# Attention and a quantised product on one core: the beginning rebuilt (decay factors by way of TensorE, first rows in halves)

## The reference

```python
q = x @ Wq; k = x @ Wk; v = x @ Wv
latent_kv = (k + v) @ W_down_kv            # 128 -> 32
k_rec = latent_kv @ W_up_k                 # 32 -> 128
v_rec = latent_kv @ W_up_v
scores = clip(einsum(qh, kh) * scale)      # scale = 1/sqrt(128)
decay = exp(-0.01 * 0.01 * abs(i - j))
scores = clip(scores * decay)
attn = softmax(scores)                     # over keys
out = (attn @ vh) @ Wo
x = x + attention(layernorm(x))
x = x + (fp8(layernorm(x) / s_in) @ fp8(kernel / s_k)) * (s_in * s_k) + bias
```

## Time and profile before

| | us |
|---|---|
| median of 3 runs (lowest, highest) | 534.98 (530.42, 535.65) |
| profiled execution, its own time | 534.09 |
| its span | 532.2 |
| TensorE busy with matmuls | 490.4 |
| ScalarE busy | 490.8 |
| VectorE busy | 280.6 |
| GpSimd busy | 218.8 |
| first exponential of scores begins at | 15.58 |

### The profile page before, as it was taken

One profiled execution on the slowest core, in us unless ns is written; L12 is line 12 of the kernel. 1 busy time (PEld: TensorE's weight loads), 2 busy tenths in 40 slices (PEclk: granted clock), 3 DMA queues, 4 the chain that ended last, 5 costly groups with the idle time before them and its releaser, 6 DMA issues.

```text
span 532.2 us, 9397 instructions
## 1 busy us (share of the span) xinstructions
PE 490.4 (92%) x3457; PEld 113.2 (21%) x3457; DVE 280.6 (53%) x641; ACT 490.8 (92%) x534; POOL 218.8 (41%) x285
## 2 busy tenths in 40 slices
PE   7799999899999999999999999999999999999961
PEld 3312111131122212221121211221111212122220
DVE  4524744455645564554744555554555645455646
ACT  3789999889999999999999999999999999999961
POOL 0889419791450229992251218993101211002110
PEclk9999999899999999999999999999999999999995
DMA  5589789837976102757967000757977000100000
GB/s 174 166 253 223 254 240 261 315 144 175 249 158 149 46 5 71 263 183 192 263 149 178 10 4 23 278 169 214 264 176 166 20 7 7 46 1 2 1 20 25
DMA packets 50467, 73.79 MB, mean 139 GB/s; under 512 B 6192, under 2 KB 29168, under 8 KB 50416
## 3 DMA queue, kind: packets, MB, share of 16 engines
q1 hardware_dynamic: 49600, 72.85, 49.5%
q10 hardware_dynamic: 816, 0.28, 0.2%
HBM read 35.40 MB, written 35.65 MB: 133 GB/s over the span
## 4 chain that ended last, share of the span: by engine, by line
PE 45%; ACT 34%; issue 9%; DVE 5%; DMA 3%; POOL 2%; SPq 1%; ACTq 0%; DVEq 0%; POOLq 0%
ACT probs L758 33%; PE ps L957 23%; PE ps L941 13%; DVE ps L1182 2%; PE ps L937 2%; PE ps L859 1%; PE ps L854 1%; PE ps L822 1%; PE ps L831 1%; DMA decay<-decay_rows 1%; PE ps L826 1%; DMA o_raw<-pv_out 1%; DMA wuv_s<-L_attn_W_up_v 1%; SPq L453 0%; POOL sq L584 0%
## 5 line engine op out<-in xcount | busy, mean ns | idle before, releaser
L758 ACT ACTIVATE probs<-ps 128x1024 f32<-128x1024 f32 x512 | 480.2, 1067 | 14.9 <-DVE ps L1182 9.4
L957 PE MATMUL ps<-probs,V 128*9 128x512 f32 x2048 | 268.6, 596 | 3.0 <-ACT probs L758 0.8
L1182 DVE TENSOR_TENSOR ps<-ps,consts 128x256 f32<-128x256 f32 (+1 forms) x256 | 143.9, 565 | 176.3 <-PE ps L941 169.3
L941 PE MATMUL ps<-Qs,Ks 64*128 64x512 bf16 x992 | 181.7, 386 | 16.6 <-ACT probs L758 8.4
L941 PEld LDWEIGHTS ps<-Qs,Ks 64*128 64x128 bf16 x992 | 43.9, 93 | 288.8 <-ACT probs L758 272.1
L645 POOL TENSOR_TENSOR xs<-xs,magic 128x512 f32<-128x512 f32 x7 | 8.9, 1277 | 96.2 <-DVE magic L1243 96.2
L957 PEld LDWEIGHTS ps<-probs,V 128*9 128x9 f32 x2048 | 31.3, 88 | 77.9 <-issue 57.6
L1190 DVE COPY pv_out<-ps 105x512 f32<-105x512 f32 x31 | 21.4, 691 | 33.7 <-PE ps L957 33.7
L562 POOL TENSOR_SCALAR rs<-mv 128x4 f32<-128x4 f32 (+1 forms) x10 | 2.3, 229 | 82.7 <-DVEq L1364 82.0
L596 POOL TENSOR_TENSOR sq<-sq,parts 128x1024 f32<-128x1024 f32 (+1 forms) x16 | 29.0, 1813 | 1.3
L598 POOL TENSOR_TENSOR parts<-sq,parts 128x1024 bf16<-128x1024 f32 (+1 forms) x16 | 28.3, 1771 | 1.3
(11 more groups left out here) (148 smaller groups left out, 284.7 us busy)
## 6 DMA issues: line engine op xcount, KB each, us to landing
Qs<-qp_dram SPq DMA_DIRECT2D x26, 512.0 KB, 9.2
qp_dram<-parts SPq DMA_DIRECT2D x14, 768.0 KB, 4.6
Ks<-kp_dram SPq DMA_DIRECT2D x26, 384.0 KB, 5.5
kp_dram<-parts SPq DMA_DIRECT2D x12, 384.0 KB, 3.5
kp_dram<-parts SPq DMA_DIRECT2D x6, 768.0 KB, 5.2
qp_dram<-parts SPq DMA_DIRECT2D x7, 512.0 KB, 6.0
X<-L_attn_x SPq DMA_DIRECT2D x10, 256.0 KB, 3.3
Qs<-qp_dram SPq DMA_DIRECT2D x10, 256.0 KB, 9.5
```

Source lines behind the costliest of these rows:

```text
L758: nc.scalar.activation(probs[:, quad % RING, 2 * jp:2 * jp + 2, :].rearrange("p j n -> p (j n)"), ps_all[:, bank * CH:(bank + 2) * CH], AC ...
L941: last = nc.tensor.matmul(bank, Ks[half, g, jp, key_cols(v, kc)], Qs[half, g, jp, qh, v, :], start=True, stop=True)
L957: last = nc.tensor.matmul(pv[32 * j:32 * j + VW, :], V[:, unit // 2 * NB + kc, HG * j + g, :], probs[:, quad % RING, j, :], start=i == 0, ...
L1182: nc.vector.tensor_tensor(own, own, factors, ALU.mult).then_inc(fixed, 1)
```

## The change

It touches the beginning only.

- `decay` is no longer spread by two broadcast loads. One row of 2048 factors is loaded to one partition (`factors`, which lies in the tile `probs`; `factors_in`), as the third issue of SyncE's queue. TensorE multiplies it with a row of 128 ones in three pieces of 512 columns (f32, one row deep), and ScalarE copies the three accumulators to `decay` (`spread_factors` on both engines; `factors_ps`, `decay_ready`). The fourth piece, needed only by GpSimd's `late_keys`, is still a broadcast load, of 256 KB instead of 1 MB (`decay_in`).
- The first four row tiles arrive as two loads, one on SyncE's queue and one ahead of the weights on ScalarE's (`x_quarter`). They get moments, square root, inversion and normalisation of their own, ahead of the second four; the last two tiles of the second four are normalised between `first_queries` and `first_keys`.
- `keep_busy` is 8 instead of 11, and those of 3 and 5 are gone.
- The table of the exponential is loaded after the copy of the first `xnT` and the third `spread_factors`, and the square root of the second four rows stands before that copy. The two late weight loads of ScalarE's queue move behind it.
- `load_x(1)` waits for `consts` instead of for `decay`.
- TensorE waits for the third copy of factors before slot 1, since it writes over its accumulator.

```diff
@@ sync
-            sp.dma_start(X[:, 0, 0:4, :], x_t[:, 0:4, :]).then_inc(x_half, 16)
+            sp.dma_start(X[:, 0, 0:2, :], x_t[:, 0:2, :]).then_inc(x_quarter[0], 16)
             sp.dma_start(X[:, 0, 4:NB, :], x_t[:, 4:NB, :]).then_inc(x_in[0], 16)
+            sp.dma_start(factors[:, :], decay_rows[:, :]).then_inc(factors_in, 16)
...
-            for half in range(2):
-                cols = slice(half * CH, (half + 1) * CH)
-                sp.dma_start(decay[:, :, cols], decay_rows.rearrange("o (a n) -> o a n", a=2)[:, :, cols]
-                             .broadcast_to([P, 2, CH])).then_inc((decay_half, decay_in)[half], 16)
-            sp.wait_ge(decay_half, 16)
-            sp.wait_ge(decay_in, 16)
+            sp.dma_start(decay[:, 1, CH:S], decay_rows[:, S + CH:2 * S].broadcast_to([P, CH])).then_inc(decay_in, 16)
+            sp.wait_ge(const_in, 16)
             load_x(1)
@@ gpsimd
-            pool.wait_ge(decay_in, 16)
+            pool.wait_ge(decay_ready, 3)
             pool.wait_ge(k_sb, 2)
...
             split(0, CH, CH)
+            pool.wait_ge(decay_in, 16)
             late_keys(0)
@@ scalar
+            act.dma_start(X[:, 0, 2:4, :], x.rearrange("(t p) d -> p t d", p=P)[:, 2:4, :]).then_inc(x_quarter[1], 16)
             act.dma_start(wkT_s[:, :], wkT[:, :]).then_inc(w_in, 16)
...
-            deviation(0, mv, rs)
+            def spread_factors(i):
+                v, half = FACTORS[i]
+                act.wait_ge(factors_ps, i + 1)
+                nc.scalar.copy(decay[:, v, half * CH:(half + 1) * CH], ps[:, 1 + i, :]).then_inc(decay_ready, 1)
+
+            deviation(0, mv[:, first_rows, :], rs[:, :, first_rows])
+            spread_factors(0)
+            spread_factors(1)
             act.wait_ge(fold_pe, 1)
             nc.scalar.copy(wdown_T[:, :], ps[0:DL, 7, 0:D]).then_inc(fold_act, 1)
-
-            nc.scalar.activation(unread[:, 1:2], ones[:, :], ACT.Exp, scale=SCALE)
             act.wait_ge(fold_pe, 2)
             nc.scalar.copy(wk_eff[:, :], ps[:, 6, 0:D]).then_inc(fold_act, 1)
             nc.scalar.copy(wv_eff[:, :], ps[:, 6, D:2 * D]).then_inc(fold_act, 1)
+            deviation(1, mv[:, second_rows, :], rs[:, :, second_rows])
+            act.wait_ge(tr_ps, 1)
+            nc.scalar.copy(xnT[:, 0:CH], ps[:, 4, :]).then_inc(xnT_ready, 1)
+            spread_factors(2)
+            nc.scalar.activation(unread[:, 1:2], ones[:, :], ACT.Exp, scale=SCALE)
@@ tensor
+            def spread_factors(i):
+                at = FACTORS[i][0] * S + FACTORS[i][1] * CH
+                nc.tensor.matmul(ps[:, 1 + i, :], one_row[:, :], factors[:, at:at + CH], start=True,
+                                 stop=True).then_inc(factors_ps, 1)
+
             pe.wait_ge(tiles_clear, 1)
-            keep_busy(11)
+            keep_busy(8)
+            pe.wait_ge(factors_in, 16)
+            spread_factors(0)
+            spread_factors(1)
...
-            keep_busy(3)
+            spread_factors(2)
...
-            keep_busy(5)
@@ vector
-            dve.wait_ge(x_half, 16)
-            tile_stats(0, range(4))
+            for i in range(2):
+                dve.wait_ge(x_quarter[i], 16)
+                tile_stats(0, range(2 * i, 2 * i + 2))
+            tile_moments(range(4))
+            settle()
+            dve.sem_inc(var_ready, 1)
             dve.wait_ge(x_in[0], 16)
             tile_stats(0, range(4, NB))
-            tile_moments(range(NB))
+            invert_deviation(0, mv[:, first_rows, :], rs[:, :, first_rows])
+            normalise_first(range(4)).then_inc(xn_ready[0], 1)
+            tile_moments(range(4, NB))
             settle()
             dve.sem_inc(var_ready, 1)
-            invert_deviation(0, mv, rs)
+            invert_deviation(1, mv[:, second_rows, :], rs[:, :, second_rows])
+            normalise_first(range(4, 6))
...
-            dve.wait_ge(decay_half, 16)
+            dve.wait_ge(decay_ready, 2)
             dve.wait_ge(const_in, 16)
             dve.wait_ge(q_ps, 1)
             first_queries(PLUS, ps[:, 6, :])
+            normalise_first(range(6, NB)).then_inc(xn_ready[1], 1)
             dve.wait_ge(k_ps, 1)
```

More of the change, by code:

```diff
@@ L217, in build @@
         ones = sb("ones", [P, 1])
+        factors = probs[0:1, 3, :, :].rearrange("p j n -> p (j n)")
+        one_row = sb("one_row", [1, P])
         eps = sb("eps", [P, 1])
@@ L236, in build @@
         x_in = [sem(f"x_in{b}") for b in range(B)]
-        x_half = sem("x_half")
+        x_quarter = [sem(f"x_quarter{i}") for i in range(2)]
         w_in = sem("w_in")
@@ L241, in build @@
         wq_in = sem("wq_in")
-        decay_half = sem("decay_half")
+        factors_in = sem("factors_in")
+        factors_ps = sem("factors_ps")
+        decay_ready = sem("decay_ready")
         decay_in = sem("decay_in")
@@ L350, in emptied @@
             return {"turn": turned, "n": tops_ready, "flags": oks_ready, "flag": flag_ready}[kind], i + 1
+        first_rows, second_rows = slice(0, 4), slice(4, NB)
+        FACTORS = ((0, 0), (1, 0), (0, 1))
         block = ctx.enter_context(nc.Block())
@@ L730, in _ @@
             nc.scalar.copy(wv_eff[:, :], ps[:, 6, D:2 * D]).then_inc(fold_act, 1)
+            deviation(1, mv[:, second_rows, :], rs[:, :, second_rows])
[3 more added lines that the diff above has]
+            nc.scalar.activation(unread[:, 1:2], ones[:, :], ACT.Exp, scale=SCALE)
             act.dma_start(wo_s[:, :], wo[:, :]).then_inc(late_in, 16)
             act.dma_start(w8_s[:, :], w8[:, :]).then_inc(late_in, 16)
-            act.wait_ge(tr_ps, 1)
-            nc.scalar.copy(xnT[:, 0:CH], ps[:, 4, :]).then_inc(xnT_ready, 1)
             act.wait_ge(km0_ready, 2)
@@ L767, in _ @@
                 nc.scalar.copy(OT[:, LAST % 2, half_cols[half]], ps[:, 2 + half, 0:HALF]).then_inc(ot_halves[half][0], 1)
-            deviation(1, mv2, rs2)
+            deviation(2, mv2, rs2)
             for half in range(2):
@@ L975, in _ @@
                 for s in (2 * quad, 2 * quad + 1):
+                    if s == 1:
+                        pe.wait_ge(decay_ready, 3)
                     if s == 2:
@@ L1108, in _, with normalise_first @@
             nc.vector.memset(eps[:, :], EPS)
+            nc.vector.memset(one_row[:, :], 1.0)
             nc.vector.memset(ones[:, :], 1.0).then_inc(tiles_clear, 1)
-            dve.wait_ge(x_half, 16)
-            tile_stats(0, range(4))
+            def normalise_first(tiles):
+                for t in tiles:
+                    last = nc.vector.tensor_scalar(X[:, 0, t, :], X[:, 0, t, :], mv[:, t, 0:1], rs[:, 1, t:t + 1],
+                                                   ALU.subtract, ALU.mult)
+                return last
+            for i in range(2):
[4 more added lines that the diff above has]
+            dve.sem_inc(var_ready, 1)
             dve.wait_ge(x_in[0], 16)
             tile_stats(0, range(4, NB))
-            tile_moments(range(NB))
+            invert_deviation(0, mv[:, first_rows, :], rs[:, :, first_rows])
+            normalise_first(range(4)).then_inc(xn_ready[0], 1)
+            tile_moments(range(4, NB))
             settle()
             dve.sem_inc(var_ready, 1)
-            invert_deviation(0, mv, rs)
+            invert_deviation(1, mv[:, second_rows, :], rs[:, :, second_rows])
             dve.sem_inc(stats_ready, 1)
[L1119 to L1123, removed]
+            normalise_first(range(4, 6))
             def first_keys(g, v, cols, src):
@@ L1388, in _ @@
                 if quad == 0:
-                    dve.wait_ge(decay_in, 16)
+                    dve.wait_ge(decay_ready, 3)
                     dve.wait_ge(k_ps, 2)
@@ L1430, in _ @@
             dve.sem_inc(var_ready, 1)
-            invert_deviation(1, mv2, rs2)
+            invert_deviation(2, mv2, rs2)
             for half in range(2):
```

## The result

| | before | after |
|---|---|---|
| median, us (runs) | 532.8 (14) | 537.46 (14) |
| lowest to highest | 530.42 to 535.65 | 535.07 to 541.15 |
| ratio of after to before | | 1.0075, 95% interval 1.0056 to 1.0095 |
| profiled execution, span | 534.09, 532.2 | 538.53, 536.7 |
| first exponential | 15.58 | 20.93 |

What follows compares the result with a forecast made beforehand. Matmuls and exponentials bound the long middle; only the first exponential (15.58 us) could move. Queries 0.95 us earlier, 0.53 given back, netted 0.4 us: 533.7 on the profiled basis, 534.1 from the executions' middle of 534.5; range 529.8 to 536.5.

Steps and rivals of the forecast that it cites:

- TensorE isn't free: TensorE's in-order queue at the start: factors' products at 0.86 us each and folds put the transposes at F + 3.75.
- F: Landing time of the row of factors at the start: bounded at 4.5 to 5.7 us, taken as 5.4.
- Rival A: Beginning on TensorE: factors' products, folds and transposes at half clock after an idle stretch, +4.0 us, 538.5; chance 0.12.
- The sum at full clock: Beginning at F = 5.4: transposes at 9.15 to 9.2, first exponential 0.4 us earlier, at 15.2.
- The two tiles between Q0 and K0: VectorE normalises the two last tiles between first_queries and first_keys: 0.53 us given back.
- The 0.58 us of the load: VectorE's wait for decay's broadcast before first_queries: 0.58 us beyond the next limit, gained by removing the load.
- The exponential's table: ScalarE's table load of 1.28 us near 11 us: covered with 1.4 us to spare, costed at nothing.
- Queues on which nothing waits: 768 KB less broadcast and earlier load_x(1) free queues nothing waits on in the first 16 us; costed at nothing.
- I add nothing: The middle is chained to the first exponential and moves by the same 0.4 us; nothing added.
- rival C: Near 100 us: a shifted start could miss the stall at the gather, 4.1 us less, 530.0; chance 0.18.

Runs made afterwards that it cites:

- numbers 1: Changed kernel with 11 instead of 8 products on zeros ahead of the first factors' product: 537.72 us, ratio 1.0073 to before.
- c3: Changed kernel with the first unit's sums inverted two quads later: 533.34 us, ratio 1.0024 to before.
- number 2: Changed kernel with its three one-row factors' products made 128 rows deep on zeros, so decay's factors are zeros: 533.71 us, ratio 1.0006 to before.
- c1: Kernel before with the first unit's sums inverted two quads later: 530.52 us, ratio 0.9959 to before.
- number 8: Changed kernel without spreading, all second four tiles normalised before first_queries, 2 products on zeros ahead of the transposes: 534.55 us, ratio 1.0011 to before.
- number 6: Kernel before with only the two late weight loads moved behind ScalarE's copy of xnT: 535.32 us, ratio 1.0015 to before.
- number 7: Changed kernel with 11 and 3 deep products, one-row products behind transposes and key projection, no tiles between Q0 and K0: 535.6 us, ratio 1.0027 to before.

## Why the prediction was wrong

**The step that failed** is "TensorE isn't free": "so depth buys nothing and I take 0.86 for each". Measured: two one-row products at the high level hold TensorE for 1.91 us (numbers 1 and c3), two of 128 rows for 1.92 (number 2). So depth buys no time for the product, as said; the price was only 0.1 us too low for each. What failed is that the product was priced and not what it does to the clock: with one row it leaves the clock low or lets it fall, with 128 rows it doesn't. The term was 2 x 0.86 + 0.53 + 0.86 + 0.64 = 3.75 us from F to the transposes; in after it was 12.43 - 4.88 = 7.55, in number 2, where the clock is up, 9.18 - 5.01 = 4.17.

**Rival A** had the mechanism by half (products with the factors at half clock), nearly the time (538.5; the median is 537.46, the profiled execution took 538.53) and the wrong cause. That its time came so near is partly luck: it put three products, folds and transposes at half clock, 4.4 us, and left out the projections, so it was too low for the beginning (20.93 against number 2's 15.33 is 5.6), while probably only some of the runs lose that much. It blamed an idle stretch behind the eight products, and by the earlier trace rows idling of 0.77 us had done no harm; so it got 0.12. There was no such stretch in after. In the earlier trace rows nothing excluded the true cause: all products there are 32 rows deep in four row groups at once, or deeper, apart from the two short ones of L808 and L809. What the Trainium skill (TensorE: Matmul & The Clock Gate, What's actually happening) is quoted for there, that the moment of the rise varies from run to run, agrees with the traces: about 4.6 us in before, before 4.7 in c3, about 6.6 in c1.

**F**: 5.4 was taken, between 4.5 and 5.7. In c3 TensorE waits for it until 4.91, in number 2 its first product starts at 5.01; so it was 4.9 to 5.0. The first four tiles were also ready earlier, at 7.6 and not 8.6. Both are on the gaining side.

**The sum at full clock** came out, in part by luck. Number 2 has the forecast's clock: transposes at 9.18 (forecast 9.15), queries taken up at 11.84 (11.7), K0 at 12.96 (12.85), first exponential at 15.33 (15.2). But the row of factors landed 0.4 us earlier than taken, and the road from it to the transposes was 0.4 us longer; the two cancel. The two tiles between Q0 and K0 cost about what was written; number 8 takes them back.

**The 0.58 us of the load** were read rightly from the earlier trace rows, but from one execution. In c1 and number 6 `decay` wasn't waited for at all, so against a start at 15.18 (c1) the full-clock sum gains nothing.

**The exponential's table** was covered, as costed: its load ends at 15.96 and `kT` waits until 19.02. In after the load starts 0.03 us behind the copy before it, and the next activation 0.01 us behind the load's end. So the trace doesn't show the drain that the Trainium skill (ScalarE: Activation LUTs, What ACT_TABLE_LOAD costs) adds, and the measurement decides.

**"Queues on which nothing waits"** stays open. Number 6 made it look as if the weight loads had made `decay` late, and c1 takes the ground from that.

**"I add nothing" for the middle** was too simple. The stall that rival C named exists and costs about 2 us, half of the 4.6 that C took from the runs' spread. VectorE's wait there varied from 1.3 to 3.2 us, so it adds to or absorbs what the beginning wins by up to a microsecond or so. To be rid of it took an edit of its own (c1 to c3), not a shifted start.

## What to carry to other kernels

Before a product of few rows takes the place of a warm-up product, ask what holds the clock meanwhile: put it between deep products (number 7, one execution), and read the durations of neighbours of known size, not the granted clock, to see the level. Before a load is replaced by other engines' work, look at its landing in more than one execution; here the wait that was to be saved was missing in others. A beginning's gain is only real if the next fixed rendezvous isn't set by a queue of its own; look for that first.

## What the runs showed of the hardware that I had not expected

- One-row products keep TensorE busy without a gap and still leave its clock low (3.78 us for two products, after), or let it fall from the high level (numbers 1 and c3, in the third such product, at 8.6 and 7.6 us). The same with 128 rows keep it up (number 2).
- After eleven bf16 products of 64 rows it was still low at 9.6 to 11.7 us, in a single run.
- The granted clock reads 1.00 up to the first change that is recorded, at the low level too (after, 10 to 12 us: 1.00, with one fold in 0.63 us instead of 0.38).
- The two broadcasts of `decay`, 512 KB each, took 6.6 us (median) to land in before and 5.6 in c1, with the same loads beside them.
- A table load of 1.28 us follows a copy after 0.03 us and is followed by an activation after 0.01 us (after).
